# Centring two of four layer norms through the weights, and a row's own features by matmul, in a fused graph network

## The reference

```python
x = layernorm(x + attention(x, adj))        # four heads of 16, scores masked by adj, softmax, relu
A = adj + eye                               # layer 1: mean over the neighbours, a node's own row once more
x = layernorm(x + (A @ x) / A.sum(axis=2))
x = layernorm(x + adj @ (x @ weight) + bias)          # layer 2
t = adj @ x                                           # layer 3
x = layernorm(x + where(t > 0.5, 1, 0))
```

## Time and profile before

| | us |
|---|---|
| three runs | 1648.21, 1647.0, 1645.42 |
| median | 1647.0 |
| span of the profiled execution, first to last instruction | 1639.9 |

### The profile page before, as it was taken

One profiled execution on the slowest core, in us unless ns is written; L12 is line 12 of the kernel. 1 busy time (PEld: TensorE's weight loads), 2 busy tenths in 40 slices (PEclk: granted clock), 3 DMA queues, 4 the chain that ended last, 5 costly groups with the idle time before them and its releaser, 6 DMA issues.

```text
span 1639.9 us, 22202 instructions
## 1 busy us (share of the span) xinstructions
PE 1428.8 (87%) x7728; PEld 705.3 (43%) x7728; DVE 1329.8 (81%) x1657; ACT 1243.4 (76%) x1475; POOL 1077.2 (66%) x575
## 2 busy tenths in 40 slices
PE   5897879998998899998889998988899889899766
PEld 3443434444444444444444444444444444345323
DVE  2887878888887888888888788888888788988865
ACT  2697878787887879877787778878788787887731
POOL 3367767766777666677676667777677766767422
PEclk9999999999999999999999999999999999999867
DMA  6523251313423053121513234131342304100000
GB/s 101 69 41 45 46 67 33 46 31 55 55 51 44 20 72 54 42 32 40 78 27 50 25 60 62 37 43 29 55 55 51 44 21 62 39 13 14 26 10 10
DMA packets 57277, 72.02 MB, mean 44 GB/s; under 512 B 23878, under 2 KB 44878, under 8 KB 57166
## 3 DMA queue, kind: packets, MB, share of 16 engines
q0 software_dynamic: 13824, 18.01, 14.6%
q1 hardware_dynamic: 42142, 51.97, 12.9%
q10 hardware_dynamic: 1200, 0.63, 0.2%
HBM read 102.87 MB, written 3.26 MB: 65 GB/s over the span
## 4 chain that ended last, share of the span: by engine, by line
PE 48%; DVE 23%; ACT 12%; issue 11%; DMA 2%; POOL 1%; SPq 1%; ACTq 1%; DVEq 0%; POOLq 0%
PE M L612 11%; DVE RUN L855 10%; PE M L561 9%; PE Z L522 9%; PE Z L524 8%; ACT LS L703 6%; ACT LS L711 3%; PE Z L535 3%; DVE LS L869 3%; PE Z L622 3%; PE Z L683 2%; PE Z L570 1%; DVE X L960 1%; DVE RUN L852 1%; DVE RSTD L948 1%
## 5 line engine op out<-in xcount | busy, mean ns | idle before, releaser
L429 POOL TENSOR_TENSOR LS<-LS,MB 125x1000 f32<-125x1000 f32 x372 | 861.3, 2332 | 413.2 <-DVE LS L869 322.4
L855 DVE TENSOR_TENSOR RUN<-Z,RUN 125x1000 f32<-125x1000 f32 x528 | 631.5, 1196 | 197.5 <-ACT LS L703 186.5
L703 ACT ACTIVATE LS<-Z 125x1000 f32<-125x1000 f32 x576 | 575.2, 999 | 196.9 <-PE Z L524 195.6
L711 ACT ACTIVATE LS<-LS 125x1000 f32<-125x1000 f32 x576 | 595.1, 1034 | 45.5 <-POOL LS L429 24.3
L522 PE MATMUL Z<-AT,BI 126*125 126x500 fp8e4 x1152 | 377.1, 409 | 99.0 <-DVE RUN L855 85.9
L561 PE MATMUL M<-LS,V 125*18 125x500 f32 x2304 | 317.3, 624 | 43.4 <-ACT LS L711 42.6
L524 PE MATMUL Z<-FS,FO 96*125 96x500 bf16 x1152 | 354.7, 390 | 0.0
L869 DVE TENSOR_TENSOR LS<-LS,MB 125x1000 f32<-125x1000 f32 x204 | 286.9, 1411 | 8.2 <-DMA MB<-row_maxima 1.7
L522 PEld LDWEIGHTS Z<-AT,BI 126*125 126x125 bf16 x1152 | 136.1, 141 | 242.6 <-DVE RUN L855 154.2
L524 PEld LDWEIGHTS Z<-FS,FO 96*125 96x125 bf16 x1152 | 162.3, 141 | 107.4 <-issue 14.2
L612 PE MATMUL M<-AT,XP 125*128 125x500 fp8e4 x756 | 203.3, 391 | 0.0
(11 more groups left out here) (120 smaller groups left out, 1003.7 us busy)
## 6 DMA issues: line engine op xcount, KB each, us to landing
MB<-row_maxima SPq DMA_DIRECT2D x48, 500.0 KB, 3.8
A<-in_adj_dram POOLq DMA_DIRECT2D x96, 183.1 KB, 4.8
FO<-PARTS SPq DMA_DIRECT2D x192, 46.9 KB, 2.1
FS<-PARTS SPq DMA_DIRECT2D x180, 46.9 KB, 2.1
XP<-in_x_dram SPq DMA_DIRECT2D x8, 336.0 KB
XA<-in_x_dram SPq DMA_DIRECT2D x8, 336.0 KB
out_dram<-X SPq DMA_DIRECT2D x7, 375.0 KB
row_maxima<-LMAX SPq DMA_DIRECT2D x48, 3.5 KB
```

Of the source, the lines that this page charges most:

```text
L429: nc.gpsimd.tensor_tensor(rows, rows, MB[:P, u % 2, :, :], ALU.subtract).then_inc(sub_pool, 1)
L703: nc.scalar.activation(LS[:P, q % RL, :, :], banks("Z", q)[:P], ACT.Prelu, alpha=0.2).then_inc(bent, 1)
L711: nc.scalar.activation(rows, rows, ACT.Exp, scale=0.25).then_inc(exps, 1)
L855: nc.vector.tensor_tensor(run, z, run, ALU.max).then_inc(maxed, 1)
```

## The change

The mean over features is taken out of two norms. Norm 1's input is `x + (sum + x) / count`, in which `x` is a norm's result; norm 2's is `x + sums @ w2 + bias`. The identity (for norm 3 it stays as it was), `w2` and the bias are centred over the output feature once before the loop, so that what comes back for norm 1 or 2 has mean zero already, and `mean`, `centre` and `centred` are called for norms 0 and 3 alone. `WW` now has a third part: 2 is the centred identity (layer 1), 1 the centred `w2` (layer 2), 0 the plain identity (layer 3). DVE works out the row sums and centred parts ahead of its main loop, after the constants; PE waits for them (`wc_ready`), and for a 16-bit copy of the identity that ACT makes (`id_ready`).

A row's own features, which POOL's `prepare` multiplied in, enter layer 1's collection by four more matmuls for each slice (`own_rows`): a tile of `XP` as weights, the 16-bit identity's 125 columns moving, into 125 of the bank's 500 columns each. Layer 2's bias enters its turned result by one more matmul for each slice (`bias_rows`): the 32-bit identity as weights, the bias repeated over 256 columns moving. `prepare`, `end_prepare`, the third step of `neighbours` and their semaphores are gone; DVE adds to `X` instead of to a prepared `Y`. ACT's square for norms 1 and 2 waits for the last addition (`added`) instead of the centring.

```diff
-CONSTS = 16 + RS - 1
-LINKS = 4 * 3
+CONSTS = 19 + RS - 1
+CENTRED = (0, 3)
+MIXES = (2, 1, 0)
+BEFORE = (0, 3, 4, 5)
+LINKS = 8
...
-NEIGHBOURS = {26: 0, 27: 1, 30: 2}
+NEIGHBOURS = {26: 0, 27: 1}
...
-            const(nc.gpsimd.memset(WW[:, 0, :], 0.0))
-            for c in range(2):
-                diagonal(WW[:, 0, :], F * c, F, 1.0)
+            for w in (0, 2):
+                const(nc.gpsimd.memset(WW[:, w, :], 0.0))
+                for c in range(2):
+                    diagonal(WW[:, w, :], F * c, F, 1.0)
...
-                at = layer_at(q, BASE)
-                if at and at[1] < 2:
-                    prepare(*at)
...
+            def own_rows(bank, c):
+
+                for k in range(ST):
+                    last = nc.tensor.matmul(bank[:, k * P:(k + 1) * P], XP[:, ST * c + k, :], ID16[:, :],
+                                            start=False, stop=(k == ST - 1))
+                return last
+
+            def bias_rows(bank):
+
+                nc.tensor.matmul(bank[:P, 0:ST * F], ID[:P, :P], B2[:, :].unsqueeze(1).to_broadcast([P, ST, F]),
+                                 start=True, stop=False)
...
-                                            start=(m == 0), stop=(m == NT - 1))
+                                            start=(m == 0), stop=(m == NT - 1 and l > 0))
+                if part == 2 and l == 0:
+                    last = own_rows(M1, c)
...
+                if l == 1:
+                    bias_rows(z[:, 0, :])
                 for k in range(ST):
                     last = nc.tensor.matmul(z[:P, 0, k * F:(k + 1) * F], YT[:, k * P:(k + 1) * P],
-                                            WW[:, 1 if l == 1 else 0, :], start=True, stop=True)
+                                            WW[:, MIXES[l], :], start=(l != 1), stop=(l != 1 or k == ST - 1))
...
+            pe.wait_ge(wc_ready, 5)
+            pe.wait_ge(id_ready, 1)
...
-                act.wait_ge(dve_seq, link_of(b, l, 1))
+                if l in CENTRED:
+                    act.wait_ge(dve_seq, link_of(b, l, 1))
+                else:
+                    act.wait_ge(added, 9 * b + 3 * l)
...
+            nc.scalar.activation(ID16[:, :], ID[:P, :P], ACT.Copy).then_inc(id_ready, 1)
...
-                if l < 2 and c == 0:
-                    dve.wait_ge(y_ready, 2 * b + l + 1)
+                if l == 0 and c == 0:
+                    dve.wait_ge(den_seq, 2 * (b + 1))
...
-                                                             in1=Y[:, t, :], op0=ALU.mult, op1=ALU.add)
+                                                             in1=X[:, t, :], op0=ALU.mult, op1=ALU.add)
                 elif l == 1:
-                    ins = nc.vector.tensor_tensor(y, ps, y, ALU.add)
+                    ins = nc.vector.tensor_tensor(y, ps, xx, ALU.add)
...
             def normalise(l, c):
-                centred(l, c)
+                if l in CENTRED:
+                    centred(l, c)
                 summed(l, c)
...
+            dve.wait_ge(weights_in, 4 * 16)
+            nc.vector.tensor_reduce(WSUM[:, 1:3], WW[:, 1:3, :], AX.X, ALU.add).then_inc(wc_ready, 1)
+            nc.vector.tensor_reduce(BSUM[:, :], B2[:, :], AX.X, ALU.add).then_inc(wc_ready, 1)
+            dve.wait_ge(wc_ready, 2)
+            for w in (1, 2):
+                nc.vector.scalar_tensor_tensor(out=WW[:, w, :], in0=WSUM[:, w:w + 1].to_broadcast([128, F]), scalar=-1.0 / F,
+                                               in1=WW[:, w, :], op0=ALU.mult, op1=ALU.add).then_inc(wc_ready, 1)
+            nc.vector.scalar_tensor_tensor(out=B2[:, :], in0=BSUM[:, :].to_broadcast([P, F]), scalar=-1.0 / F,
+                                           in1=B2[:, :], op0=ALU.mult, op1=ALU.add).then_inc(wc_ready, 1)
...
-                if layer_at(q, 0):
-                    mean(*layer_at(q, 0))
-                if layer_at(q, CENTRE):
-                    centre(*layer_at(q, CENTRE))
+                at = layer_at(q, 0)
+                if at and at[1] in CENTRED:
+                    mean(*at)
+                at = layer_at(q, CENTRE)
+                if at and at[1] in CENTRED:
+                    centre(*at)
```

More of the change, by code:

```diff
@@ L122, in adj_resnorm @@
         WA = sb("WA", [F, 2, H, D], f32)
-        WW = sb("WW", [128, 2, F], f32)
+        WW = sb("WW", [128, 3, F], f32)
+        WSUM = sb("WSUM", [128, 3], f32)
+        BSUM = sb("BSUM", [P, 1], f32)
+        ID16 = sb("ID16", [P, P], f16)
         B0 = sb("B0", [P, H, D], f32)
@@ L176, in adj_resnorm @@
         factors_in = sem("factors_in")
-        y_ready = sem("y_ready")
+        wc_ready = sem("wc_ready")
+        id_ready = sem("id_ready")
         added = sem("added")
@@ L282, in link_of @@
         def link_of(b, l, n):
-            return LINKS * b + 3 * l + n + 1
+            return LINKS * b + BEFORE[l] + (n if l in CENTRED else 0) + 1
         def by_vector(e):
@@ L482, in _ @@
                     end_power(l, c)
[L483 to L486, removed]
         @block.tensor
@@ L683, in _ @@
                             last = nc.tensor.matmul(Z[:, c, 0, 0:C], XP[:, m, :], AT[:P, (NS * (B - 1) + c) % RS, q, :, m % ST],
-                                                    start=(m == 0), stop=(m == NT - 1))
+                                                    start=(m == 0), stop=(m == NT - 1 and l > 0))
+                        if q == NS - 1 and l == 0:
+                            last = own_rows(Z[:, c, 0], c)
                         if q == NS - 1:
@@ L690, in _ @@
                     pe.wait_ge(end_taken, 3 * l + c + 1)
+                    if l == 1:
+                        bias_rows(Z[:, c, 1])
                     for k in range(ST):
                         last = nc.tensor.matmul(Z[:P, c, 1, k * F:(k + 1) * F], parts[c][:, k * P:(k + 1) * P],
-                                                WW[:, 1 if l == 1 else 0, :], start=True, stop=True)
+                                                WW[:, MIXES[l], :], start=(l != 1), stop=(l != 1 or k == ST - 1))
                     last.then_inc(end_back, 1)
@@ L924, in neighbours @@
                     return
-                dve.wait_ge(den_seq, 3 * b + n)
-                if n == 1:
-                    nc.vector.reciprocal(RDEN[:, :], DEG[:, :]).then_inc(den_seq, 1)
-                else:
-                    nc.vector.tensor_scalar(RDEN1[:, :], RDEN[:, :], 1.0, None, ALU.add).then_inc(den_seq, 1)
+                dve.wait_ge(den_seq, 2 * b + n)
+                nc.vector.reciprocal(RDEN[:, :], DEG[:, :]).then_inc(den_seq, 1)
             def rows_of(l):
@@ L994, in add @@
                 dve.wait_ge(end_back, 3 * l + c + 1)
-                if l < 2:
-                    dve.wait_ge(end_base, 3 * l + c + 1)
+                dve.wait_ge(end_x, 3 * l + c + 1)
                 bank = Z[:, c, 1]
@@ L1002, in add @@
                         ins = nc.vector.scalar_tensor_tensor(out=Y[:, t, :], in0=ps[:, k, :], scalar=RDEN[:, t:t + 1],
[L1003 removed]
+                                                             in1=X[:, t, :], op0=ALU.mult, op1=ALU.add)
                 elif l == 1:
[L1005 removed]
+                    ins = nc.vector.tensor_tensor(y, ps, X[:, ST * c:ST * (c + 1), :], ALU.add)
                 else:
@@ L1091, in _ @@
                 if q == LAST_ROWS:
-                    for n in range(3):
+                    for n in range(2):
                         neighbours(B - 1, n)
```

12 lines of the change are left out of this document (removed).

## The result

The changed kernel takes 1635.57 us (median of 4 runs, 1631.12 to 1638.34), the kernel before beside it 1647.61 (4 runs): ratio 0.9922, interval 0.9897 to 0.9947. Weighted by their runs that is 0.9936, or 10.5 us less. The forecast was 4.2 us less: the sign was right, the size too small by more than half.

A forecast was written before the change was run, and what follows sets the result against it. PE was taken to bound the collecting stretches, DVE the normalising ones. A graph: +0.78 + 1.50 - 1.73 - 0.95 = -0.40 us; seven graphs -2.8, tail -1.4, total -4.2 us: 1642.8 us, range 1635 to 1652.

The forecast's parts named there:

- Norm 1, -1.73 a graph: Layer 1's normalising on DVE: removing mean (0.87 us) and centring (0.86 us) saves 1.73 us a graph.
- norm 2, -0.95: Layer 2's normalising on DVE: removing the mean saves 0.1 us, the centring 0.86, together 0.95 us a graph.
- nothing late takes the place: Norm 1: ACT's square then waits only for the last sum, there before ACT comes, so the full 1.73 us is won.
- Own rows, +0.78: Layer 1 on PE: 12 pairs of weight load and 125-column matmul at 0.065 us each add 0.78 us a graph.
- Rival 2: Own-row pairs cost what 32-bit pairs cost, 0.10 to 0.14 us each: 1646 to 1650 us, no change; chance 0.24.
- Bias, +1.50: Layer 2 on PE: three 32-bit matmuls of 256 columns at 0.50 us each add 1.50 us a graph, in full.
- POOL's bases at nothing: Removing POOL's two prepared bases (1993 and 2208 ns a graph) gains nothing, as PE has no gap they could have caused.
- Tail, -1.4: Last graph, after the loop: PE's additions against DVE's savings and one small count step less, together -1.4 us.
- rival 3: Less idling after layer 1's normalising keeps PE's clock up in five graphs: 7.5 us won, 1635.3 us; chance 0.12.
- Rival 1, the lock: DVE's subtraction in layer 1's norm waits up to 1.3 us a graph for POOL's port lock: 1651.9 us; chance 0.14.
- Some 7 us outside the span: Runs' median 1647.0 against profiled span 1639.9 was taken to leave some 7 us outside the span, untouched by the change.
- the start: Before the loop: DVE's centring of weights and bias, about 1.3 us, is hidden by 0.4 us before PE starts.

The follow-up runs named there:

- the kernel that has both: Changed kernel with layer 1's base also prepared on POOL and later overwritten, own rows kept on PE: 1638.84 us, ratio 0.9936 (0.9918 to 0.9953).

## Why the forecast was wrong, and which of its terms held

The sign was right and the mechanism held: DVE's stretches shorten, PE's lengthen. The size was wrong, 4.2 us forecast and 10.5 measured. The step that failed is the price of PE's additions, 0.78 + 1.50 us a graph "in full", which measured 0.70 + 0.98; after it comes the tail, -1.4, which measured -2.6.

- *Norm 1, -1.73 a graph; norm 2, -0.95.* Right in size: -1.64 and -0.93. DVE sets the end of the first. But "nothing late takes the place" did not hold there: the chain runs over ACT until 706.40, and that goes with the 0.09 that are missing. In the second ACT's bend leaves only the centring's 0.86 and a little, as the prediction had it.
- *Own rows, +0.78.* Nearly right: 0.055 us a pair in a row and 0.70 a graph, below the value taken (0.065). The Trainium skill ("TensorE: Matmul & The Clock Gate", section "Back-to-back issue gap") gives about 81 ns for each pair in a stream of them; by it, as an estimate, the 12 pairs would take 0.97 us, and the trace disagrees. Rival 2, pairs at 0.10 us or more, is out.
- *Bias, +1.50.* Here the forecast failed, in the step "Both additions lie in stretches where PE has no gap, so they count in full". One bias is 0.43 us, not 0.50, and the third is not in the collecting: it comes at the first bend of norm 2, where PE waits. It cost 0.98 a graph. With the smaller own rows, less the 0.11 that the norms fell short, this is the 0.48 us by which a graph's sum was off, 3.4 us over seven.
- *POOL's bases at nothing.* Right for layer 1, by the kernel that has both. Layer 2's was not tried by itself.
- *Tail, -1.4.* The instructions gave that, -1.30. What failed is what was left out: the clock, which the prediction weighed in the loop alone (rival 3). The tail won -2.6. The third collecting ran at 1.00 in all four executions of the change, after 1.95 or 1.96 us of idling, and fell in both of before, after 3.83. The shorter wait alone doesn't decide that: with norm 1's centring kept, and in one execution without own rows, the wait is as short and the clock falls (0.82 and 0.85), so why it kept is not shown. The same collecting in these two:

```profile
1632.35 9.72 PE L682 MATMUL Z<-AT,XP 125*128 125x500 fp8e4 x36 [1.96 <-DVE XP L1053]
```

```profile
1618.95 9.39 PE L703 MATMUL Z<-AT,XP 125*128 125x500 fp8e4 x36 [1.95 <-DVE XP L1078]
```

- *Rival 1, the lock.* Did not happen: 1.19 or 1.20 us in all seven graphs.
- *Rival 3 in the loop.* Did not happen in the change itself. Steps 49 to 52 take 8.60 us on average in two executions of before and 9.09 in four of after, so falls are no fewer. The prediction had them blur the sum by 2 or 3 us; between the executions of before and after the steps left out differ by 5.8, and without own rows graph after graph meets the same falls in two of three executions.
- *The base.* "Some 7 us outside the span" was wrong: it is 1.8, and the execution profiled lies at the low end. As the forecast is a difference, that did not move it.

Of the missing 6.3 us (10.5 less 4.2), 3.4 are the additions of the loop, 1.2 the tail, 0.1 the start. The last 1.6 are within the uncertainty; by the line above 0.9 of them would be the clock's.

The experiments also point to a version that beats both kernels: folding alone, with POOL keeping both bases (0.9883 and 0.9903).

## What to carry to other kernels

Price a trade between engines stretch by stretch, and check for each added instruction, not for each kind, in which stretch it lands: the last of a series can fall into the next one, as the third bias did. Where the clock falls now and then, cut the trace into steps and use those that repeat at one clock; judge the rest by runs, with the mean clock beside the time. Give work to an engine that waits (POOL here) rather than to the one that bounds its stretch, and measure the loan alone before joining it with the saving.

## What the hardware showed that was not expected

- Runs of one unchanged kernel differ by up to 1.3% (1641.6 to 1663.3 us over 105 runs), and the mean granted clock (0.936 to 0.952) goes with it.
- In the tail PE waits 1.95 or 1.96 us for its third collecting in eleven executions of all kernels: nine ran it at the full clock (8.02 us in that of after), two fell (9.72 and 9.39). After 2.8 us or more, in eight executions, the clock always fell (9.98 us in that of before, mean 0.78).
- Matmuls of 12 columns in PE's gaps didn't keep its clock: in the graph shown the fall came with 0.35 us of idling left of 0.88, and the mean clock of the runs hardly moved (0.949 against 0.946).
- One 0.22 us group of four small matmuls, three times a graph, goes with a mean clock of 0.946 instead of 0.941, and the 0.70 us of PE time a graph that leaving it out saves never showed in the time.
